# GpSimd adds the two halves before LayerNorm's mean and variance products

## What is computed

```python
x = x + ffn(cond(x, side, lens, ...), ...)      # DEPTH = 2 layers in ffn
# one layer:
h = shift_token(x); q, k, v = split(h @ wqkv)
q = l2norm(q) * qs; k = l2norm(k) * ksc; q, k = rotary_xpos(q, k)
x = x + local_attention(q, k, v) @ wo           # 8 heads of 64, window 128
h = shift_token(x)
mu = h.mean(-1); var = h.var(-1)
h = (h - mu) / sqrt(var + 1e-05) * lg + lb      # the LayerNorm of this change
a, g = split(h @ w1 + b1)
x = x + (a * gelu(g)) @ w2 + b2
```

## Time and profile before

| what | value |
|---|---|
| median of 3 runs | 4105.37 us (4104.72 to 4107.03) |
| the profiled execution, its own time | 4102.22 us |
| its span in the trace | 4100.1 us |
| mean granted TensorE clock | 0.969 |
| PE busy | 3832.6 us, 93% |
| DVE busy | 2793.1 us, 68% |
| ACT busy | 2343.0 us, 57% |
| POOL busy | 786.1 us, 19% |

### The profile page before, as it was taken

How to read it: one execution, slowest core, us unless ns; L and a number is a source line. 1 busy time by engine, 2 the same in 40 slices (tenths; PEclk the granted TensorE clock), 3 DMA queues, 4 the chain that set the end, 5 groups by cost and what they waited for, 6 DMA issues and landing times.

```text
span 4100.1 us, 70276 instructions
## 1 busy us (share of the span) xinstructions
PE 3832.6 (93%) x22372; PEld 2562.4 (62%) x22372; DVE 2793.1 (68%) x7663; ACT 2343.0 (57%) x5248; POOL 786.1 (19%) x976
## 2 busy tenths in 40 slices
PE   6799999999999999999999999999999999999987
PEld 3456666666666666666666666666666666666655
DVE  3577677667677767677767767767767767767653
ACT  2355556655656655656655656655656655656552
POOL 1122122112122112122112122212122212122100
PEclk6799999999999999999999999999999999999997
DMA  3000000000000000000000000000000000000000
GB/s 116 6 11 7 5 11 11 11 11 6 6 11 11 11 11 6 6 11 11 11 11 6 6 11 11 11 11 6 6 11 11 11 11 6 6 11 6 6 6 8
DMA packets 48277, 46.55 MB, mean 11 GB/s; under 512 B 8716, under 2 KB 46816, under 8 KB 48096
## 3 DMA queue, kind: packets, MB, share of 16 engines
q1 hardware_dynamic: 48096, 44.87, 3.5%
HBM read 35.69 MB, written 8.39 MB: 11 GB/s over the span
## 4 chain that ended last, share of the span: by engine, by line
PE 40%; issue 38%; DVE 11%; POOL 7%; ACT 2%; DVEq 0%; POOLq 0%; DMA 0%; SPq 0%; ACTq 0%
PE ps L981 6%; POOL inv L549 5%; PE ps L876 5%; PE ps L890 4%; PE ps L734 4%; PE ps L952 3%; PE ps L932 2%; PE ps L943 2%; PE ps L791 2%; PE ps L816 2%; PE ps L923 2%; PE ps L910 1%; DVE feed_area L1260 1%; DVE attn_area L1190 1%; DVE ssq L1194 1%
## 5 line engine op out<-in xcount | busy, mean ns | idle before, releaser
L981 PE MATMUL ps<-feed_area,w_s 128*128 128x256 f32 x2560 | 595.2, 384 | 7.4 <-DVE feed_area L1262 6.3
L549 POOL TENSOR_TENSOR inv<-ssq_f,minus_half 128x16 f32<-128x16 f32 x128 | 419.2, 3275 | 946.3 <-DVE ssq_f L1198 946.3
L647 ACT ACTIVATE attn_area<-attn_area,f_nb,inv 128x128 f32<-128x128 f32 (+1 forms) x1024 | 546.1, 538 | 22.7 <-DVE f_nb L1226 21.9
L981 PEld LDWEIGHTS ps<-feed_area,w_s 128*128 128x128 f32 x2560 | 479.2, 192 | 92.9 <-issue 16.8
L1135 DVE TENSOR_REDUCE c_mx<-ps 128x2 f32<-128x512 f32 x512 | 343.6, 688 | 142.2 <-PE ps L763 138.9
L600 ACT ACTIVATE cond_area<-ps 128x512 f32<-128x512 f32 x512 | 299.2, 598 | 240.3 <-PE ps L781 232.8
L1222 DVE CUSTOM_DVE_ANT_0 attn_area<-ps,cst 128x128 f32<-128x128 f32 (+1 forms) x1024 | 304.1, 353 | 148.3 <-issue 148.3
L1272 DVE SCALAR_TENSOR_TENSOR feed_area<-ps,b_s,feed_area 128x256 f32<-128x256 f32 (+1 forms) x384 | 184.5, 481 | 268.1 <-ACT feed_area L669 262.1
L994 PE MATMUL ps<-feed_area,w_s 128*128 128x256 f32 x1536 | 355.3, 381 | 0.7 <-DVE feed_area L1272 0.7
L638 ACT ACTIVATE attn_area<-ps 128x512 f32<-128x512 f32 x256 | 152.9, 597 | 323.3 <-PE ps L910 320.5
L669 ACT ACTIVATE feed_area<-ps,b_s 128x256 f32<-128x256 f32 x320 | 150.9, 472 | 311.6 <-PE ps L981 311.2
(11 more groups left out here) (150 smaller groups left out, 7113.1 us busy)
## 6 DMA issues: line engine op xcount, KB each, us to landing
x_rows<-in_x SPq DMA_DIRECT2D x32, 256.0 KB, 2.7
f_rows<-in_fside_BxSxS SPq DMA_DIRECT2D x32, 256.0 KB, 3.0
res_rows<-in_x SPq DMA_DIRECT2D x32, 256.0 KB, 2.8
out<-res_rows SPq DMA_DIRECT2D x32, 256.0 KB, 2.6
wqkv_s<-in_L_ffn_wqkv SPq DMA_DIRECT2D x2, 1536.0 KB
w_s<-in_L_ffn_w SPq DMA_DIRECT2D x2, 1364.0 KB
cond_area<-cond_area SPq DMA_DIRECT2D x128, 6.0 KB
w_s<-in_L_ffn_w SPq DMA_DIRECT2D x2, 640.0 KB
```

The source lines that it names most:

```text
L549: nc.gpsimd.tensor_tensor(inv[:, l, t, :], ssq_f[:, l, t, :], minus_half[:, :], ALU.pow).then_inc(SL[l]["inv_norm"], 1)
L647: nc.scalar.activation(soft[:, h % SOFT, lo:hi], soft[:, h % SOFT, lo:hi], ACT.Exp, bias=f_nb[:, l, q, h:h + 1], scale=inv[:, l, q, h:h + ...
L981: last = mm(ps[:, N0 + f % 2, c * N:(c + 1) * N], w1_s[:, l, k, lo:lo + P], hn[:, k, :], start=(k == 0), stop=(k == KD - 1))
```

## The change

GpSimd gets two steps per layer. In `mean` it adds the two halves of the shifted `X_attn` into `xsum` (which shares its columns with `rstd_s`); in `variance` it adds the two halves of `hsq` into `hsum` (shared with `std_s`). TensorE then makes one product with `mean_w` in place of two in each step, and waits for GpSimd's sum in place of VectorE's or ScalarE's result. New semaphores are `x_added` and `dev_added`.

```diff
+    x_added=1, mean=1, centered=1, dev_squared=1, dev_added=1, variance=1, std=1,
...
-        std_s = feed.take(N)
-        rstd_s = feed.take(N)
+        hsum = std_s = feed.take(N)
+        xsum = rstd_s = feed.take(N)
...
+                elif name == "mean":
+                    both = shifted(X_attn[l])
+                    pool.wait_ge(SL[l]["x_attn"], upto(seq, "x_attn", KD))
+                    was = previous(l, seq)
+                    if was:
+
+                        pool.wait_ge(SL[was[0]]["normed"], upto(was[1], "normed", 1))
+                    nc.gpsimd.tensor_tensor(xsum, both[:, 0, :], both[:, 1, :], ALU.add).then_inc(SL[l]["x_added"], 1)
+                elif name == "variance":
+
+                    pool.wait_ge(SL[l]["dev_squared"], upto(seq, "dev_squared", 1))
+                    nc.gpsimd.tensor_tensor(hsum, hsq[:, 0, :], hsq[:, 1, :], ALU.add).then_inc(SL[l]["dev_added"], 1)
...
-                    for k in range(KD):
-                        last = mm(ps[:, N0, 0:N], mean_w[:, :], shifted(X_attn[l])[:, k, :],
-                                  start=(k == 0), stop=(k == KD - 1))
-                    last.then_inc(SL[l]["mean"], 1)
+                    pe.wait_ge(SL[l]["x_added"], upto(seq, "x_added", 1))
+                    mm(ps[:, N0, 0:N], mean_w[:, :], xsum, start=True, stop=True).then_inc(SL[l]["mean"], 1)
                 elif name == "variance":
-                    pe.wait_ge(SL[l]["dev_squared"], upto(seq, "dev_squared", 1))
-                    for k in range(KD):
-                        last = mm(ps[:, N0 + 1, 0:N], mean_w[:, :], hsq[:, k, :], start=(k == 0), stop=(k == KD - 1))
-                    last.then_inc(SL[l]["variance"], 1)
+                    pe.wait_ge(SL[l]["dev_added"], upto(seq, "dev_added", 1))
+                    mm(ps[:, N0 + 1, 0:N], mean_w[:, :], hsum, start=True, stop=True).then_inc(SL[l]["variance"], 1)
...
-    Pool=((54, 11, 29, 1),
+    Pool=((65, 16, 22, 0),
```

More of the change, by code:

```diff
@@ L129 @@
     DVE=((65, 16, 22, 0),
-        "RSSRRRNSRRASAASARSSRSSSASSAANASASASSAAAARSRASSAASSNNRNSRANNAARSARNSSSRNNRNRAAARARRANAAASRSSNNNAAANNA"
+        "RSSRRRNSRRASAASARSSRSSSASSAANASASASSAAAARSRASSAASSNNRNRASNNAARSARNSSSRNNRNRAAARARRANAAASRSSNNNAAANNA"
         "NAARSANSSASNASASAAASAAAAASSAASASSAAASSSSAASSAAASAAAAARANAAARA"),
     Activation=((57, 19, 24, 0),
-        "AAAAAARARARRARASNSASASSASRSAAAAANASSSAARSARSRRASNSSNASSRAANRSSSSNNASANRASNNARAAARNAAARAANARSSNNRNSNA"
+        "AAAAAARARARRARASNSASASSASRSAAAAANASSSAARSARSRRASNSSNASSARANSRSSSNNASANARSNNAARAANRAAAARANASRSNNNRSNA"
         "NAAANSAANASRSASASAANASSAASAAAASNASRRRASSSSSAAARASSSRSAASAASAS"),
-    Pool=((54, 11, 29, 1),
-        "NNSNNRRRRRRRRRRRNNNSSNNNSNSSSSSSASASASSASAAAAAAAAASSNNNNAAAAAASSRSSNNNAANSSAAAAARNNSSAASSSSSSSRRRSSS"
-        "SSAAAAAAAAAAARRRRSAAAAAAAAASSSASSASSSRRRRAAAAAAAAAAAAAAAAAASS"),
+    Pool=((65, 16, 22, 0),
+        "NRSSRRRSRRASAASARSSRSSSASSAANASASASSAAAASRSRASSAANSNNNSRANAARRSARNSSSRNNRNRAAARARRANAAASRSSNNNANNANA"
+        "ARSANAASSASNASASAAASAAAAASSASSSASSAAAASSAASSAAASAAARRAAANAAAA"),
 )
@@ L183 @@
     pv=FH, o_copied=HP, wo_out=KD, x_attn=KD,
-    mean=1, centered=1, dev_squared=1, variance=1, std=1,
+    x_added=1, mean=1, centered=1, dev_squared=1, dev_added=1, variance=1, std=1,
     rstd=1, normed=1, w1_out=HK, gelu=HK, geglu=HK,
@@ L543, in layer @@
             def layer(seq, name, n):
-                if name != "rotate":
+                if name == "finish":
                     return
                 l, t = n[0:2]
-                pool.wait_ge(SL[l]["floored"], upto(seq, "floored", t + 1))
-                nc.gpsimd.tensor_tensor(inv[:, l, t, :], ssq_f[:, l, t, :],
-                                        minus_half[:, :], ALU.pow).then_inc(SL[l]["inv_norm"], 1)
+                if name == "rotate":
+                    pool.wait_ge(SL[l]["floored"], upto(seq, "floored", t + 1))
+                    nc.gpsimd.tensor_tensor(inv[:, l, t, :], ssq_f[:, l, t, :],
+                                            minus_half[:, :], ALU.pow).then_inc(SL[l]["inv_norm"], 1)
+                elif name == "mean":
[8 more added lines that the diff above has]
+                    nc.gpsimd.tensor_tensor(hsum, hsq[:, 0, :], hsq[:, 1, :], ALU.add).then_inc(SL[l]["dev_added"], 1)
             def step(seq, name, n):
@@ L955, in layer @@
                 elif name == "mean":
-                    pe.wait_ge(SL[l]["x_attn"], upto(seq, "x_attn", KD))
                     was = previous(l, seq)
```

## The result

The change made the kernel slower: 4211.87 us in the median of four runs (4200.6 to 4212.23) against 4105.05 us before (4095.52 to 4107.03), a ratio of 1.026 with a 95% interval of 1.024 to 1.028. The forecast, 4086 us with a range to 4113, was wrong, in sign and in size. The profiled execution took 4211.97 us, its span 4209.9. One execution of a later kernel, the changed one with the head filled, took 6409.73 us at a mean granted clock of 0.555 and is left out of its ratio.

The account below looks back on a forecast made before the run. TensorE, busy 93%, bounds the kernel through its own work plus waits. Passes 0.34 us shorter give 10 us and the clock 9: 19 off 4102.2 gives 4083, or 4086 at the median; range 4064 to 4113.

Parts of the forecast that it names:

- part 1: TensorE makes one product fewer in 128 places, 0.43 us each; gains and waits weighed at four places of a pass.
- variance, layer 1: TensorE starts at 1948.22 instead of 1947.53, waiting for GpSimd's sum; layer 1 as a whole loses 0.26 us per pass.
- The loss bound of 0.85 us per pass: Layer 1's worst case: its second sum held 0.6 us behind VectorE's copies L1128.
- Part 4, the clock: Passes 0.34 us shorter escape the half-clock stretch more often: 5.5 more free passes, 9 us gained, bounds 0 and 14.
- the new half-clock stretch: Rival, 9%: longer sums make TensorE idle around layer 1's LayerNorm, costing 1.6 us in each of 29 passes: 4141 us.
- 20% case: No-change rival, 20%: layer 1's second sum held 0.6 us behind copies L1128; time stays between 4097 and 4112 us.
- Layer 0's mean: Sum ready at least 2.1 us early even if held, so no wait; gain 0.17 us, bounds 0 and 0.43.
- Layer 0's variance: Sum ready 8.6 us before TensorE comes, so no wait; gain 0.43 us, bounds 0.3 and 0.43.
- Layer 1's mean: Sum stands behind GpSimd's power instruction; TensorE waits 0.30 us, saves 0.43, and is free 0.13 us sooner.
- The root behind the variance: Layer 1: ScalarE loads a table after the variance in any case and the root waits for that, so delay is covered.
- Moved steps: Power instruction ahead of GpSimd's branch and swaps on ScalarE and VectorE: costed at nothing.
- Outside the loop: Twelve of the 128 places lie outside the 29 passes; put at zero, bounds 3 us either way.

Follow-up runs that it names:

- head filled: Seven products of constants ahead of TensorE's wait at the head of a pass: changed kernel 4117.67 us, kernel before 4059.73 us.
- layer 1's wait filled: Changed kernel plus four products of constants ahead of TensorE's wait for layer 1's variance: 4132.22 us, ratio 1.008.
- the hold taken away: Changed kernel, with VectorE's key multiplication L1220 made to wait for layer 1's second sum: 4090.92 us, ratio 0.998.

## Why the prediction was wrong

The loss, by the passes of the kernels above, in us per pass, clock left out: layer 0's two sums -0.53 (121.06 to 120.53, heads filled); layer 1's mean -0.01 (to 120.52); layer 1's variance with a sum of 0.73 us +0.34 (to 120.86); the hold of that sum by L1220 +0.92 (120.86 to 121.78). Together +0.72. Then the clock: 126.29 - 121.78 = 4.51 us of half clock where the kernel before has 122.53 - 121.06 = 1.47, +3.04. Over 29 passes 21 us are waits, less what the products save, and 88 us are clock.

- **The step that failed** stands in part 1, under variance, layer 1: "I take 0.26: L1128 reads PSUM, and the row of a held operation is one beside an instruction with two SBUF inputs." The rule about neighbours was right, and the neighbour was the wrong one. I looked at who is on VectorE when the sum starts and not at who comes next. In the earlier trace rows L1128, twice, starts at 1946.74 and VectorE was said to be at it until 1948.02. What follows it is L1212, the same key multiplication with two SBUF inputs; I had not looked for it, and no row of mine holds it. In the trace of before it starts at 1947.93:

```profile
1947.53 1.13 PE L969 MATMUL ps<-feed_area,mean_w 128*128 128x256 f32 x4 [0.17 <-ACT feed_area L658]
1947.93 0.68 DVE L1212 TENSOR_TENSOR attn_area<-attn_area,inv 128x512 f32<-128x512 f32 x1
```

  The sum was forecast from 1947.42 to 1948.15, so it overlaps. The Trainium skill (GPSIMD Engine Reference, Specifications) has the rule that an instruction with two SBUF inputs on VectorE contends with GpSimd, and the trace agrees: 1.64 us beside L1220, 0.73 without. The loss bound of 0.85 us per pass was for a sum held 0.6 us; it was held for 0.91, and layer 1 lost 0.34 + 0.92 - 0.01 = 1.25 us of a pass, where the forecast had 0.26.
- **Part 4, the clock, had the wrong sign.** Its mechanism was a slide: shorter passes get past the half-clock stretch sooner. That is what the kernels with shorter passes do (with sums in layer 0 alone, 9 of the 27 regular passes are free of the stretch, where before three were). But the pass became longer, the wait at the variance brought a stretch of its own, and the head's came at all 28 starts. My 9 us of gain were 88 of loss. The term rested on the pass being shorter and on there being one stretch, so it fell with the step above.
- **The rival that came true** is the new half-clock stretch, given 9%. It named the place, the kind of wait and the condition, "if the sums take 0.6 to 1 us longer". Its price, 1.6 us in each pass less the 10 us gained, missed two things. The head's stretch became dearer too: both cost 4.5 us, where layer 1's alone costs 1.68 in the passes that have it (head filled) and the head's alone 123.69 - 121.78 = 1.9 (layer 1's wait filled). And the hold costs 0.92 on its own. It gave 4141 and not 4212. I treated the rival as independent of the hold, when a hold that was a 20% case in its own right would also bring it; the two belonged together.
- **With the hold taken away the time lies in the forecast's own range**: 4090.9 us measured, 4086 forecast; the wait 0.98 us, about 1 forecast; no half clock around it. The gain is half of the forecast's, 10 us for 19. A pass is shorter by 0.20 us and not by 0.34, since layer 0 gives 0.53 for 0.60 and layer 1's mean 0.01 for 0.13, while the variance costs 0.34 for 0.39.
- **Layer 0's mean.** Its sum is held, as the worse bound had it, and is there long before TensorE asks: no wait, right. **Layer 0's variance:** no wait: right.
- **Layer 1's mean.** The sum starts behind the power instruction and lasts 0.72 us, as forecast. But VectorE's subtraction starts 0.78 us behind the start of the product, where it was 1.15: the single product brings the chain 0.37 us and not 0.43, and the wait takes that.
- **The root behind the variance** was said to be covered by ScalarE's table load. It was in the trace of before; now the load ends at 1996.57 and the root waits until 1997.27 for the product.
- **Moved steps** at nothing: right (1.000). **Outside the loop** at zero with bounds of 3 us: not shown. Outside the 27 lengths the changed kernel's profiled execution takes 799.8 us against 791.8, and the two passes of the loop in it account for 7.5 of the 8; but the kernels with the head filled lie between 787 and 800 there, so a few us can't be told.
- **What would show it wrong** had "a wait of over 1.6 us at layer 1's variance, or PEclk below 1.00 around it". It was 1.89, and 0.54.

## What to carry to other kernels

When work goes to GpSimd, walk VectorE's queue over the whole time the new operation lasts, the instruction behind the present one included: one with two SBUF inputs that starts part of the way through lengthened a 0.73 us sum to 1.64 here. A wait of TensorE has two prices, its length and what the clock does behind it, and the second was the larger here, 88 us of 109; where TensorE must wait, cheap products of constants that fit within the wait give the clock back (41 us in the kernel before, 94 in the changed one). Take the halves of a change apart before judging it: the layer with room to spare gained 30 us alone; the bare one cost 58 alone and 137 on top of the other (4074.47 to 4211.87).

## What the hardware showed that I had not expected

- **Same wait, two outcomes.** An idle time of 1.89 us was followed by half clock in 17 of 28 passes and by full clock in the others of one execution, with the same instructions around it; 1.45 and 0.98 us were followed by it in no pass of the loop. The 3.17 us at the head were followed by it at 25 of 28 starts in the kernel before, and at 18 of 28 with layer 0's sums alone. It isn't chance from pass to pass: behind the first two, no two neighbouring passes of the 28 were free of it. So one measured pass without half clock doesn't clear the wait before it.
- **The prices of two half-clock stretches in a pass don't add up.** With sums in layer 1 alone, both came in every second pass and neither in the others; with layer 0's sums added, and a pass 0.5 us shorter, both came in all 28. With that 0.5 us saved came 50 us of loss (4162.28 to 4211.87), where the same saving in the kernel before came with a gain of 30. Why the pattern locks in one case and alternates in the other stays open: no run here separates the phase of a pass from the time between the two waits.
- **How long a held operation takes.** Both the sum beside L1220 (0.68 us) and the one beside L1198 (1.21 us) took 1.64 us and ended about 0.6 us after their neighbour, one begun 0.37 us ahead of it and the other 0.16 behind. So the hold goes by the neighbour's end: an operation that has already begun is held as well, and the neighbour isn't (L1220 takes the 0.68 us that L1212 took with no sum beside it). These are two cases of one size; the 8 columns of L522 ended 0.05 us behind their neighbour, so the 0.6 us are not a constant.
